# Two layers of attention and experts in one program: transposes for the value sums, and another place for the additions of expert rows

## The reference, cut to what matters

```python
qkv = hidden_states @ qkv_w.T + qkv_b            # 16 heads of 16 numbers
scores = jnp.einsum('bqhd,bkhd->bhqk', q, k) * scale
scores = jnp.where(causal[None, None], scores + bias[None], NEG)
attn = jax.nn.softmax(scores, axis=-1)
s = jnp.einsum('bhqk,bkhd->bqhd', attn, v).reshape(b, s, d) @ out_w.T + out_b
...
top_vals, top_idx = jax.lax.top_k(logits, TOP_K)     # 2 of 8 experts for each row
routing = jax.nn.softmax(top_vals, axis=-1)
out = out + ye * we[:, None]                         # ye: an expert's rows, we: its weight
...
x = x + s * silu(out)
```

## Time and profile before

| | us |
|---|---|
| median of 3 runs | 846.91 |
| lowest and highest | 841.86, 848.41 |
| the profiled execution | 845.22 |
| its span, first to last instruction | 843.4 |
| PE busy in the span | 714.2 |
| DVE busy | 585.0 |
| ACT busy | 476.7 |
| POOL busy | 156.5 |

### The profile page before, as it was taken

How to read it: one execution, slowest core, us unless ns; L and a number is a source line. 1 busy time by engine, 2 the same in 40 slices (tenths; PEclk the granted TensorE clock), 3 DMA queues, 4 the chain that set the end, 5 groups by cost and what they waited for, 6 DMA issues and landing times.

```text
span 843.4 us, 14515 instructions
## 1 busy us (share of the span) xinstructions
PE 714.2 (85%) x5342; PEld 335.0 (40%) x5342; DVE 585.0 (69%) x1190; ACT 476.7 (57%) x990; POOL 156.5 (19%) x297
## 2 busy tenths in 40 slices
PE   3477788868889998999998899989999988988885
PEld 1244454433334444444443444444444432333333
DVE  5999776598677766776777677767767777874121
ACT  2277767641566656655656555556556566546551
POOL 1422350047500001001000100010000007620111
PEclk9689989875799999999999999999999998769998
DMA  9710326534352532353247325322522412320001
GB/s 296 253 39 0 94 70 194 185 128 151 141 113 62 120 112 70 87 127 81 71 133 138 88 74 118 106 70 84 126 85 70 125 56 83 106 114 1 26 26 50
DMA packets 76994, 85.84 MB, mean 102 GB/s; under 512 B 34313, under 2 KB 60428, under 8 KB 76556
## 3 DMA queue, kind: packets, MB, share of 16 engines
q1 hardware_dynamic: 71114, 74.05, 30.9%
q0 software_dynamic: 3280, 8.98, 3.4%
q10 hardware_dynamic: 2530, 1.89, 0.8%
HBM read 39.56 MB, written 27.53 MB: 80 GB/s over the span
## 4 chain that ended last, share of the span: by engine, by line
PE 58%; ACT 15%; DVE 9%; issue 7%; DMA 4%; POOL 3%; SPq 2%; ACTq 2%; POOLq 0%; DVEq 0%
PE bank L1534 16%; PE bank L1470 8%; ACT PR L802 7%; PE bank L1432 7%; PE bank L1493 5%; PE bank L1442 5%; PE bank L1304 4%; PE bank L1549 4%; DVE PM L1203 3%; PE bank L1347 2%; PE bank L1575 2%; DMA OPS<-qk_parts 2%; ACT U L791 2%; POOL XT L567 2%; ACTq L783 2%
## 5 line engine op out<-in xcount | busy, mean ns | idle before, releaser
L802 ACT ACTIVATE PR<-bank 128x512 f32<-128x512 f32 (+3 forms) x640 | 317.6, 537 | 253.6 <-PE bank L1493 146.7
L1203 DVE TENSOR_REDUCE PM<-bank 128x1 f32<-128x512 f32 (+3 forms) x640 | 354.6, 603 | 74.4 <-PE bank L1470 46.9
L1493 PE MATMUL bank<-OPS 57*128 57x512 f16 (+3 forms) x640 | 211.8, 368 | 52.9 <-ACT PR L802 47.1
L1470 PE MATMUL bank<-OPS 54*128 54x512 f16 (+3 forms) x640 | 198.1, 379 | 11.6 <-DVE PM L1203 8.2
L1534 PE MATMUL bank<-PR,VS 128*17 128x512 f32 (+3 forms) x1280 | 164.0, 565 | 0.0
L1493 PEld LDWEIGHTS bank<-OPS 57*128 57x128 f16 x640 | 52.9, 94 | 119.4 <-ACT PR L802 110.3
L1470 PEld LDWEIGHTS bank<-OPS 54*128 54x128 f16 x640 | 50.3, 96 | 119.5 <-DVE PM L1203 75.1
L535 POOL TENSOR_TENSOR NP<-NM,NIL 128x8 bf16<-128x8 f32 x32 | 7.6, 239 | 462.2 <-DVE NM L1211 462.0
L1432 PE MATMUL bank<-WB 128*128 128x256 f16 x552 | 80.6, 275 | 0.0
L1432 PEld LDWEIGHTS bank<-WB 128*128 128x128 f16 x552 | 46.4, 101 | 35.9 <-issue 29.4
L1503 PE MATMUL bank<-MASK 64*128 64x64 bf16 x512 | 59.7, 199 | 0.0
(11 more groups left out here) (179 smaller groups left out, 780.6 us busy)
## 6 DMA issues: line engine op xcount, KB each, us to landing
WB<-W SPq DMA_DIRECT2D x23, 512.0 KB, 3.5
OPS<-qk_parts SPq DMA_DIRECT2D x60, 192.0 KB
x_rows<-PR SPq DMA_DIRECT2D x23, 256.0 KB, 3.2
WB<-in_w SPq DMA_DIRECT2D x23, 256.0 KB, 3.5
y_rows<-XT SPq DMA_DIRECT2D x23, 256.0 KB, 2.7
W<-in_w SPq DMA_DIRECT2D x6, 512.0 KB, 7.5
XT<-in_b SPq DMA_DIRECT2D x23, 128.0 KB, 3.7
XO<-in_x SPq DMA_DIRECT2D x4, 512.0 KB, 12.8
```

The source lines that it names most:

```text
L802: act.activation(PR[:, tile % RING, off:CH], PS[2 + tile % 2][:, off:CH], ACT.Exp, scale=1 / SCORE).then_inc(b_exped, 1)
L1203: dve.tensor_reduce(PM[:, c % 2, j, xq, gg:gg + 1], bank[:, 0:width], AX.X, ALU.max).then_inc(a_reduced, 1)
L1470: last = mm(bank[:, 0:width], OPS[ROWS_A, slot, 0, P * (TC * a + xq):P * (TC * a + xq) + P], OPS[ROWS_A, slot, 1, CH * gg:CH * gg + width] ...
L1493: last = mm(bank[:, off:CH], OPS[ROWS_B, slot, 1, P * k:P * k + P], OPS[ROWS_B, slot, 0, CH * b + off:CH * b + CH], start=True, stop=k < T ...
```

## The change

1. heads_out turns U by four transposes with the identity IDN into all 512 columns of bank 7. The two key halves then lie side by side, and DVE adds them with a reduction (gather_groups) into a new buffer HS in SBUF. inverse and divide read HS. Bank 7 is given back after this reduction (o_summed) and not after the division. SEL is gone.
2. Each of the 16 gathers has its own buffer: GB now lies over W1, which the experts have done with by then, and no gather waits for an addition. On POOL the gathers stand at steps of their own (GATHER_AT, every four steps from 564).
3. The additions stand at steps 630, 633 and so on to 675.
4. POOL's list is now made by a loop over the steps. In it all scatters from tile 6 on stand ahead of the third chunk's maxima.

```diff
-ADD_AT = {FIRST_BLOCK + EVERY * BLOCKS + 24 + 3 * n: t
+ADD_AT = {TOTAL - 10 + 3 * n: t
           for n, t in enumerate([2 * q + r for q in END_PAIRS for r in range(2)])}
-GATHERS = 5
+GATHERS = NT
+GATHER_AT = {PER_PAIR * (PAIRS - 1) + 4 + 4 * n: n for n in range(NT)}
+VALUES_AT = {PER_PAIR * p + LEAD + LAG + 3: p for p in range(1, PAIRS - 1)}
...
-        GB = xt32[:, 1024:1024 + 512 * GATHERS].rearrange("p (g a d) -> p g a d", g=GATHERS, a=2)
+        GB = W1[:, :, :].rearrange("p a n -> p (a n)").bitcast(F32).rearrange("p (g a d) -> p g a d", g=GATHERS, a=2)
...
-            return ((mt_copied, o_normed, ye_copied)[kind], m + 1)
+            return ((mt_copied, o_summed, ye_copied)[kind], m + 1)
...
-            scatter(range(6, 11))
-            maxima(2)
-            scatter(range(11, NT))
-            maxima(3)
...
+            scatter(range(6, NT))
+
+            for n in range(LEAD, STEPS):
+                ended = ends_of(n) if n < TOTAL else None
+                if ended is not None:
+                    maxima(ended)
+                if n in VALUES_AT:
+                    p = VALUES_AT[n]
                     pool.wait_ge(pv_done, PER_PAIR // QUADS * p)
                     head_values(2 * p + 2)
                     head_values(2 * p + 3)
-                maxima(NC * p + 3)
+                if n in GATHER_AT:
+                    gather(GATHER_AT[n])
...
+            groups = PS[7][:, :].rearrange("p (q j r w) -> p q j w r", q=TC, j=2, r=2)
+
+            def gather_groups(m):
+
+                dve.wait_ge(o_ps, m + 1)
+                dve.tensor_reduce(HS[:, m % 2], groups[:, :, :, 0:HD + 1, :], AX.X, ALU.add).then_inc(o_summed, 1)
+
             def inverse(m):
 
-                dve.wait_ge(o_ps, m + 1)
-                dve.reciprocal(RC[:, m % 2, :, :], outputs[:, :, :, HD:HD + 1].rearrange("p q j c -> p q (j c)")).then_inc(o_rc, 1)
+                dve.wait_ge(o_summed, m + 1)
+                dve.reciprocal(RC[:, m % 2, :, :], HS[:, m % 2, :, :, HD:HD + 1].rearrange("p q j c -> p q (j c)")).then_inc(o_rc, 1)
...
                 for q in range(TC):
-                    wide = 2 * HD + 2
-                    last = mm(PS[7][:, wide * q:wide * q + wide], U[:, m % 2, P * q:P * q + P], SEL[:, :],
-                              start=True, stop=True)
+                    last = pe.transpose(PS[7][:, P * q:P * q + P], U[:, m % 2, P * q:P * q + P], IDN[:, :])
                 last.then_inc(o_ps, 1)
```

More of the change, by code:

```diff
@@ L112, in build @@
 def build(nc, x, w_qkv0, w_out0, w_ffn, b_ffn, w_qkv1, b_qk1, b_v1, w_out1, b_out1, slopes, pos_rows, pick,
-          masks, ident, sel, table, gate_w, gate_b, w1, b1, w2, b2, out):
+          masks, ident, table, gate_w, gate_b, w1, b1, w2, b2, out):
     ctx = ExitStack()
@@ L143, in build @@
         IDN = sb("IDN", [P, P])
-        SEL = sb("SEL", [P, 2 * HD + 2])
         MV = sb("MV", [P, NT, 2])
@@ L169, in build @@
         RC = sb("RC", [P, 2, TC, 2])
+        HS = sb("HS", [P, 2, TC, 2, HD + 1])
         GW = sb("GW", [P, KK, E])
@@ L297, in build @@
         half_added = sem("half_added")
+        o_summed = sem("o_summed")
         rows_zero, x_scattered, y_added = sem("rows_zero"), sem("x_scattered"), sem("y_added")
@@ L558, in scatter, with gather @@
                             in_=XT[:, t % TC // 2, t % 2, CH * (t // TC):CH * (t // TC) + CH], in_offset=None).then_inc(x_scattered, 16)
[L560 to L570, removed]
+            def gather(n):
+                if n == 0:
+                    for par in range(2):
+                        pool.wait_ge(y_stored[par], 16 * ((BLOCKS + 1 - par) // 2))
+                t = list(ADD_AT.values())[n]
+                for a in range(2):
+                    pool.indirect_dma_start(
+                        out=GB[:, n, a, :], out_offset=None, in_=y_rows,
+                        in_offset=bass.IndirectOffsetOnAxis(ap=SLOT[:, a, t:t + 1], axis=0)).then_inc(y_gathered[n], 16)
             pool.wait_ge(sorting, PLACED)
@@ L611, in _ @@
             act.dma_start(IDN[:, :], ident).then_inc(const_in, 16)
-            act.dma_start(SEL[:, :], sel).then_inc(const_in, 16)
             for n, bias in enumerate((b_ffn, b_out1, b_v1, gate_b)):
@@ L1122, in add_experts @@
                 place = list(ADD_AT).index(n)
-                dve.wait_ge(y_gathered[place % GATHERS], 32 * (place // GATHERS + 1))
-                dve.tensor_scalar(ACC[:, t, :], GB[:, place % GATHERS, 0, :], WTS[:, 0, t:t + 1], None, ALU.mult)\
+                dve.wait_ge(y_gathered[place], 32)
+                dve.tensor_scalar(ACC[:, t, :], GB[:, place, 0, :], WTS[:, 0, t:t + 1], None, ALU.mult)\
                     .then_inc(half_added, 1)
                 dve.wait_ge(half_added, place + 1)
-                dve.scalar_tensor_tensor(ACC[:, t, :], GB[:, place % GATHERS, 1, :], WTS[:, 1, t:t + 1],
+                dve.scalar_tensor_tensor(ACC[:, t, :], GB[:, place, 1, :], WTS[:, 1, t:t + 1],
                                          ACC[:, t, :], ALU.mult, ALU.add).then_inc(y_added, 1)
@@ L1225, in divide @@
                 dve.tensor_tensor(XO[:, TC * b:TC * b + TC, 2 * HD * p:2 * HD * p + 2 * HD].rearrange(
-                                      "p q (j c) -> p q j c", j=2), outputs[:, :, :, 0:HD],
+                                      "p q (j c) -> p q j c", j=2), HS[:, m % 2, :, :, 0:HD],
                                   RC[:, m % 2, :, :].unsqueeze(3).broadcast_to([P, TC, 2, HD]), ALU.mult)\
@@ L1271, in _ @@
                         dve.wait_ge(x1_spill, 16 * NC)
+                    gather_groups(m)
                     inverse(m)
@@ L1277, in _ @@
                     end_product(END_AT[n - 4])
+            gather_groups(NC * PAIRS - 1)
             inverse(NC * PAIRS - 1)
@@ L1349, in back @@
                     last.then_inc(s_ps, 1)
-            pe.wait_ge(const_in, 32)
+            pe.wait_ge(const_in, 16)
             transposes(0, 0)
@@ L1656, in _shape_constants @@
         pick[r, 1, r // 2 if r % 2 == 1 else 3] = 1
[L1657 to L1660, removed]
     first = np.arange(E * NT) % NT == 0
@@ L1679 @@
     x, wqkv0, wout0, wf, bf, wqkv1, bqkv1, wout1, bout1, slopes, gw, gb, w1, b1, w2, b2 = a
-    table, pos_rows, pick, masks, ident, sel = _shape_constants()
+    table, pos_rows, pick, masks, ident = _shape_constants()
     w1v = w1.reshape(E, 2, P, 2, KK, P).transpose(5, 0, 3, 1, 4, 2).reshape(P, E * 1024)
```

5 lines of the change are left out of this document (2 added, 3 removed).

## The result

The changed kernel took 821.81 us (median of four runs, 819.61 to 833.77), the kernel before 845.28 beside it: a ratio of 0.9729 with a 95% interval of 0.969 to 0.9769. The ratio leaves out the longest of the four runs, which counts as slow. The forecast was 827 us, with a range of 817 to 839. The profiled execution took 819.61 us.

What follows compares the result with a forecast made beforehand. PE was taken to bound the middle, and DVE's additions, gathers before POOL's maxima and a low clock the last pair. +5.5 - 10.0 - 14.3 + 0.8 - 0.4 = -18.4 us from 845.22 gave 826.8, taken as 827; range 817 to 839.

Steps and rivals of the forecast that it cites:

- What bounds the kernel: Whole kernel: PE busy 714.2 of 843.4 us, above all in the middle; last pair held by additions, gathers and low clock.
- Value sums, 10.0 us: Heads outputs before number 26: transposes replace SEL products, PE saves 0.48 us a group, 0.40 kept, 25 groups gain 10.0 us.
- The estimate of 0.27 us for four transposes: Value sums: the skill's four times faster FP32 transposes would cost 0.27 us, 25 groups giving 20 us; not used in the sum.
- Rival A: Heads outputs: strided reduction of 0.9 us or more on DVE eats the heads' gain, 10.4 us gone, 837 us; chance 0.15.
- The third chunk's maxima behind all scatters, +5.5: Near 219 us: PE waits for POOL's maxima(2) from 219.4 to 224.9, 5.5 us lost, ends 4 and 8.
- Last pair, -14.3: Heads 26 to 30: gathers spread and additions moved, 62.0 us instead of 76.33, 14.3 gained; ends 16.1 and 5.
- Three additions among the last maxima, +0.8: Steps 630, 633, 636: 2.5 us on DVE, mostly hidden by PE's lead of three score banks; 0.8 us lost, ends 0 and 2.5.
- The tail, -0.4: Last two heads outputs: one saves 0.40 us on PE, the very last saves 0.48 and pays 0.50; 0.4 us gained.
- a sign of being wrong: End of the kernel: the tail from heads 30 to the end longer than before would speak against the forecast.
- Rival B: Last pair recovers only half: DVE full at additions from 630, a gap drops the clock, 7 us back, 834 us; chance 0.15.
- Rival C: Last pair and tail: PE's clock falls to 1.2 GHz for long, 60 us of it give 850 us, slower than before; chance 0.04.

Runs made afterwards that it cites:

- the first trace: Profiled execution of the changed kernel's first timing, all of the change against the kernel before: 819.61 us; median of its four runs 821.81 us, ratio 0.9729.
- the second trace: Profile of the changed kernel timed again without any edit, against the kernel before: median 826.81 us, ratio 0.9834; heads 30 to 32 took 56.00 us.
- the second timing: The changed kernel timed again without any edit, against the kernel before on the same chip: 826.81 us (825.54 to 836.08), ratio 0.9834.

## Why the prediction was right, step by step

- **What bounds the kernel** (PE in the middle): right. The eight traces with transposes in which the clock doesn't fall between heads 5 and 25 agree there to 0.07 us, whatever was edited elsewhere, and PE's own time (SEL, 0.425 a group) moves it.
- **Value sums, 10.0 us**: right, by two sizes that were both a little off and cancelled. The transposes take 0.65 us, not 0.60 as in the tail, so a group saves 0.43 on PE, not 0.48; but all of it is kept (0.425), not 0.40. The reduction takes 441 ns: the read with a step of 32 elements costs next to nothing over the 432 that the prediction drew from the plain rows, and the higher end of 0.61, drawn from SBUF rows, did not apply. 25 x 0.425 is 10.6; the other 2.3 of the table's 12.9 go with the two falls of the clock in the middle before, where the changed kernel has none. The term left out that the clock falls more often with SEL: undone, the transposes are worth 20 to 25 us in the whole. The estimate of 0.27 us for four transposes, which the sum did not use, set products of 34 columns beside transposes of 128 columns. Rival A needed a reduction of 0.9 us; it has 0.44.
- **The third chunk's maxima behind all scatters, +5.5**: the gap was foretold within 0.3 us in the first trace (5.74), its price was too low. The step that failed is the choice of 5.5 in "PE's two score banks give no room to run ahead", which counts the gap and nothing behind it: 7.5 and 11 us in two traces, with an upper end of 8.
- **Last pair, -14.3**: right in size (-15.4; 60.96 against 62.0 forecast). The reasons were a list of three, and the runs weigh them in part: gathers ahead of the maxima and additions among them each hold the pair by themselves, so both had to move. From both old places, moving the additions alone gains 0.8 of 9.4 us, spreading the gathers (with the additions 12 steps later) 2.8. The places and the heads make 11.1 of the 15.4 us; the other 4.3 go with the longer time at 0.50 before. By an estimate the clock weighed more there than the direct waits: at the prediction's price of 0.39 us for each us at 0.50, 37.6 us would account for nearly all of the 15.4, while PE waited directly for POOL's maxima for 2.0 us in the pair before, and for 4.8 with the gathers back. With both old places back the clock stands at 0.50 for 13.7 us of the pair; why it was 37.6 before is not shown.
- **Three additions among the last maxima, +0.8**: 0. That PE's lead in its score banks hides them is the prediction's reason, and no run isolates it.
- **The tail, -0.4**: +0.1 behind heads 32. Heads 30 to 32 gained 2.4: 0.85 for two heads outputs, and the rest with a stretch of 3.4 us at 0.50 that the first trace lacks. That part is luck: the second trace has two such stretches and 56.00 us, and from heads 30 to the end it takes 72.2 us against 71.3 before, which the prediction counted as a sign of being wrong.
- **Rival B** saw DVE nearly full at the additions, and so it is (14.75 of 16 us from 736), but no gap followed that the clock fell at: it stands at 1.00 from 688 to 752. **Rival C** was the one that spoke of the right thing. It didn't come, but the table's time at 0.50, 10 to 63 us, goes nearly in step with the span of the thirteen profiled executions, from 10.2 us at 813.2 to 61.7 us at 844.5. That alone doesn't tell cause from effect, since a wait both costs time and can be followed by a low clock.
- The Trainium skill ("TensorE: Matmul & The Clock Gate", Part 4: PE-mode transpose) has transposes not counted as busy time for the full clock. No run bears it out here: the kernels with 32 groups of transposes fell to 0.50 less often in the middle than those with products.

Against the profiled execution the sum was 7.2 us short (-18.4 for -25.6): 1.9 in the last pair with its additions, 2.9 between heads 1 and 26 and 1.9 behind heads 30, some 4 us of these with falls of the clock before that the sum left out, and 2.0 in the first layer, which the change doesn't touch, less 1.5 at the third chunk's maxima. The two terms that carry the gain came out within 8%: 10.6 for 10.0 (without the falls of the clock) and 15.4 for 14.3. That the second timing's median (826.81) meets the forecast is luck: there the late maxima cost 11 us and not 5.5.

## What to carry to other kernels

When a helper engine's queue holds both long issues (gathers, scatters) and short work that the bottleneck waits for, put the short work ahead by step, not the issues by lot; and when two things hold one stretch, move both, since undoing either takes most of the gain back. Price a gap on TensorE above what it lasts: here a gap of 5.74 us cost 7.5 to 11, and waits of 1.4 and 3.4 us in the last pair went with stretches of 6.8 and 10.2 us at 0.50. Read a gain from the same stretch of several traces, since executions of one program differ by 3 to 14 us in total and by 0.1 us or less in a stretch at the full clock.

## What the hardware showed that was not expected

In the changed kernel's trace the second instruction of an addition took 1.37 to 1.38 us in place of 0.48 wherever POOL added at the same time; DVE's timeline with and without, and POOL's:

```profile
771.43 1.37 DVE L1119 SCALAR_TENSOR_TENSOR ACC<-W,WTS,ACC 128x256 f32<-128x256 f32 x1
...
773.95 0.48 DVE L1119 SCALAR_TENSOR_TENSOR ACC<-W,WTS,ACC 128x256 f32<-128x256 f32 x1
```

```profile
771.21 1.30 POOL L598 TENSOR_TENSOR OPS<-OPS,TG 128x512 f32<-128x512 f32 x1 [7.23 <-DVE TG L1239]
```

It happened to three of sixteen, each one begun during such an addition of POOL (771.21, 777.76, 783.63), and each ended some 0.28 us after POOL's had. The Trainium skill ("GPSIMD Engine Reference", Specifications) says that the two share their SBUF interfaces, with contention for DVE instructions with two SBUF inputs; L1119 is one, and the rows agree.
